# A decoder block in fp32 on one core: keys and values of both halves made in one go and kept, heads in runs of sixteen, and a reordered opening

## What is computed

```python
x = _rmsnorm(hidden_states, ln_weight)
h_q = (x @ w_q.T).reshape(b, lq, H, DH)             # H = 32 heads, DH = 128
h_k = (key_value_states @ w_k.T).reshape(b, lk, H, DH)
h_v = (key_value_states @ w_v.T).reshape(b, lk, H, DH)
score = einsum('bqhd,bkhd->bhqk', h_q, h_k) + position_bias[None]
score = softmax(where(mask, score, -inf))
attn = einsum('bhqk,bkhd->bqhd', where(mask, score, 0), h_v).reshape(b, lq, H * DH)
return hidden_states + attn @ w_out.T
```

## Time and profile before

| | us |
|---|---|
| median of 3 runs (lowest, highest) | 774.87 (773.89, 776.28) |
| profiled execution | 773.13 |
| its span, first to last instruction | 771.3 |
| PE busy | 733.8 |
| PE weight loads busy | 578.8 |
| DVE busy | 487.1 |
| ACT busy | 399.8 |
| POOL busy | 94.9 |
| attention, about | 224 to 630 |

### The profile page before, as it was taken

How to read it: one execution, slowest core, us unless ns; L and a number is a source line. 1 busy time by engine, 2 the same in 40 slices (tenths; PEclk the granted TensorE clock), 3 DMA queues, 4 the chain that set the end, 5 groups by cost and what they waited for, 6 DMA issues and landing times.

```text
span 771.3 us, 12243 instructions
## 1 busy us (share of the span) xinstructions
PE 733.8 (95%) x4320; PEld 578.8 (75%) x4320; DVE 487.1 (63%) x841; ACT 399.8 (52%) x617; POOL 94.9 (12%) x86
## 2 busy tenths in 40 slices
PE   6999999999987999999999999999999889998993
PEld 4887888888877777777777777777776547886882
DVE  5655687577762657665576575765557737578555
ACT  5433333333345666666676656665666454554452
POOL 2010000082009000000000031000000002204503
PEclk9999999999999999999999999999999999999997
DMA  8456532546646677676776777766775333532641
GB/s 328 133 208 212 176 110 82 164 164 193 215 154 213 223 241 247 217 221 223 248 242 194 224 227 234 248 219 226 223 234 174 107 100 124 163 122 97 209 130 55
DMA packets 61335, 145.08 MB, mean 188 GB/s; under 512 B 6896, under 2 KB 6912, under 8 KB 60640
## 3 DMA queue, kind: packets, MB, share of 16 engines
q1 hardware_dynamic: 59696, 136.73, 54.9%
q0 software_dynamic: 1360, 7.23, 2.4%
q10 hardware_dynamic: 224, 0.39, 0.2%
HBM read 142.23 MB, written 2.10 MB: 187 GB/s over the span
## 4 chain that ended last, share of the span: by engine, by line
PE 87%; DVE 4%; DMA 3%; ACT 2%; issue 2%; POOL 1%; SPq 0%; ACTq 0%; DVEq 0%; POOLq 0%
PE bank L475 24%; PE acc L475 15%; PE bank L593 8%; PE acc L728 8%; PE bank L647 7%; PE bank L706 7%; PE bank L612 7%; PE bank L689 7%; DMA a_raw<-a 2%; PE bank L507 1%; PE bank L625 1%; DMA ak<-ax 1%; DVE a_lo L1111 1%; PE bank L673 1%; ACT t_ring L1005 1%
## 5 line engine op out<-in xcount | busy, mean ns | idle before, releaser
L475 PE MATMUL bank<-feat_hi,a_hi 128*128 128x512 f32 x352 | 139.2, 395 | 11.2 <-DVE feat_lo L1111 7.5
L475 PE MATMUL bank<-feat_lo,a_hi 128*128 128x512 f32 x352 | 137.8, 391 | 0.0
L1111 DVE TENSOR_TENSOR a_lo<-a_raw,a_hi 128x1024 fp32r<-128x1024 f32 (+1 forms) x45 | 55.4, 1230 | 99.2 <-ACT a_hi L876 92.8
L1339 DVE TENSOR_TENSOR score<-bank,mask_add 128x512 f32<-128x512 f32 x64 | 42.5, 684 | 114.0 <-PE bank L647 114.0
L593 PEld LDWEIGHTS bank<-few_ctx,ak 128*128 128x128 f32 x512 | 62.0, 191 | 44.6 <-issue 42.4
L475 PE MATMUL acc<-b_hi,tile_hi 128*128 128x512 f32 x224 | 87.7, 392 | 3.6 <-issue 1.9
L1005 ACT ACTIVATE t_ring<-bank 128x512 f32<-128x512 f32 x64 | 69.9, 1092 | 38.0 <-PE bank L612 38.0
L475 PEld LDWEIGHTS bank<-feat_hi,a_hi 128*128 128x128 f32 x352 | 66.6, 189 | 29.1 <-DVE a_lo L1111 10.0
L475 PE MATMUL acc<-b_hi,tile_lo 128*128 128x512 f32 x224 | 87.2, 389 | 0.0
L612 PEld LDWEIGHTS bank<-k_ring,wq 128*128 128x128 f32 x512 | 65.6, 192 | 25.2 <-issue 20.1
L475 PEld LDWEIGHTS bank<-feat_lo,a_hi 128*128 128x128 f32 x352 | 66.6, 189 | 13.6
(11 more groups left out here) (117 smaller groups left out, 1165.7 us busy)
## 6 DMA issues: line engine op xcount, KB each, us to landing
ak<-ax SPq DMA_DIRECT2D x64, 512.0 KB, 3.7
wq<-wqn SPq DMA_DIRECT2D x64, 256.0 KB, 3.9
wv<-wvh SPq DMA_DIRECT2D x64, 256.0 KB, 3.2
wo<-bx SPq DMA_DIRECT2D x64, 256.0 KB, 3.6
a_raw<-w SPq DMA_DIRECT2D x22, 512.0 KB, 4.2
a_raw<-a SPq DMA_DIRECT2D x21, 512.0 KB, 5.3
b_raw<-b SPq DMA_DIRECT2D x34, 256.0 KB, 2.7
b_raw<-w SPq DMA_DIRECT2D x22, 256.0 KB, 2.7
```

The costliest lines, as they stand in the source:

```text
L475: mm = pe.matmul(out_ap, w, x, start=start and k == 0, stop=stop and k == len(products) - 1, skip_group_check=True)
L1111: return dve.tensor_tensor(out_ap, whole, high, ALU.subtract)
L1339: dve.tensor_tensor(score[n % GH][:], bank[2][:].rearrange("p (b k) -> p b k", b=HB), mask_add[j][:, half * HB:(half + 1) * HB, :], ALU.ad ...
```

## The change

Heads run in four runs of sixteen: half 0 with heads 0 to 15, half 1 with heads 0 to 15 and then 16 to 31, half 0 with heads 16 to 31. In the first and third run (`shared`) keys and values are made for both halves at once, as three fp32r products of 256 columns instead of float32 ones of 128; the other half's are kept (`kept_k`, `kept_v`) and used sixteen heads later. In the second and fourth run PE makes none and only raises their semaphores; ACT still copies the banks.

```diff
+BLOCK = HEADS // 2
+WO_RING = 4
+FEATURES_1, FEATURES_2 = BLOCK - LEAD_T - 2, HN - 2
...
+def half_of(n):
+    return (0, 1, 1, 0)[n // BLOCK]
+def head_of(n):
+    return n % BLOCK + (0, 0, BLOCK, BLOCK)[n // BLOCK]
+def shared(n):
+    return n // BLOCK % 2 == 0
...
+ATTENDED = {2: BLOCK, 3: 3 * BLOCK, 4: HN}
...
+        kept_v = [sb(f"kept_v{i}", [P, P])[:] for i in range(BLOCK)]
+        wk_lo, wk_hi = [t[:] for t in two("wk_lo", [P, D], F32R)], [t[:] for t in two("wk_hi", [P, D], F32R)]
...
+        wqi, wk, wo = two("wqi", [P, D]), two("wk", [P, D]), [sb(f"wo{i}", [P, D]) for i in range(WO_RING)]
...
+        few_hi, few_lo = [t[:].rearrange("p w c k -> p (w c k)").rearrange("p (c k) -> p c k", c=C) for t in (a_hi[0], a_lo[0])]
+        wv_hi, wv_lo = [t[:] for t in b_hi], [t[:] for t in b_lo]
+        kept_k = [t[:, i:i + P] for t in (a_raw[1], b_raw[0], b_raw[1]) for i in range(0, t.shape[1], P)]
```

The context rows of both halves come as one tile into `a_raw[0]` and are split into `few_hi`, `few_lo`. The weights w_k and w_v of a shared head are split by ACT and DVE; the loads and their places change:

```diff
+            def load_q(n):
                 if n >= 2:
                     sp.wait_ge(t_mm, n - 1)
-                sp.dma_start(ak[n % 2][:], ax[n % HEADS]).then_inc(ak_dma[n % 2], 16)
-                sp.dma_start(wq[n % 2][:], wqn[n % HEADS]).then_inc(wq_dma[n % 2], 16)
+                sp.dma_start(wqi[n % 2][:], ax[head_of(n)][:, 0:D]).then_inc(wqi_dma[n % 2], 16)
+                sp.dma_start(wq[n % 2][:], wqn[head_of(n)]).then_inc(wq_dma[n % 2], 16)
+            def load_k(n):
+                if n >= 2:
+                    sp.wait_ge(k_mm, n - 1)
+                sp.dma_start(wk[n % 2][:], ax[head_of(n)][:, D:]).then_inc(wk_dma[n % 2], 16)
...
-                if n >= 2:
-                    sp.wait_ge(out_used, n - 1)
-                sp.dma_start(wo[n % 2][:], bx[n % HEADS]).then_inc(wo_dma[n % 2], 16)
...
+                if n >= WO_RING:
+                    sp.wait_ge(out_used, n - WO_RING + 1)
+                sp.dma_start(wo[n % WO_RING][:], bx[head_of(n)]).then_inc(wo_dma[n % WO_RING], 16)
...
             for n in range(2):
-                load_qk(n)
+                load_k(n)
+                load_q(n)
                 load_v(n)
                 load_o(n)
                 load_bias(n)
-            load_a(A30, A30 % 2, w3[0][:, 0:2 * D])
+            sp.wait_ge(a_lo_ok, A30)
+            sp.dma_start(a_raw[0][:], ctxF).then_inc(few_dma, 16)
+            for n in range(2, WO_RING):
+                load_o(n)
...
             for n in range(-LEAD_K, HN):
-                if 2 <= n + LEAD_K + 1 < HN:
-                    load_qk(n + LEAD_K + 1)
-                if n >= 2:
-                    load_o(n)
+                if 2 <= n + LEAD_T + 2 < HN:
+                    load_q(n + LEAD_T + 2)
+                if 2 <= n + LEAD_K + 2 < HN:
+                    load_k(n + LEAD_K + 2)
+                if WO_RING <= n + 2 < HN:
+                    load_o(n + 2)
                 if 2 <= n + 2 < HN:
                     load_v(n + 2)
+                if n == 2 * BLOCK:
+                    sp.wait_ge(few_lo_ok, 1)
+                    load_a(A30, A30 % 2, w3[0][:, 0:2 * D])
...
+            sp.wait_ge(t_mm, HN)
```

PE's keys, values (the same with `wv` and bank 3) and order in an iteration:

```diff
                 def keys(n):
-                    half, par = n // HEADS, n % 2
-                    pe.wait_ge(ak_dma[par], 16 * (n // 2 + 1))
+                    half, par = half_of(n), n % 2
+                    pe.wait_ge(wk_dma[par], 16 * (n // 2 + 1))
+                    if shared(n):
+                        pe.wait_ge(few_lo_ok, 1)
+                        pe.wait_ge(wk_lo_ok, shared_count(n))
                     if n == 0:
                         pe.wait_ge(hidden_ok, HALVES * F1)
                     else:
                         pe.wait_ge(k_ok, n)
+                        pe.wait_ge(kept_k_ok, shared_count(n - 1))
                     if n > LEAD_K + 1:
                         pe.wait_ge(u_ok, n - LEAD_K - 1)
+                    if few and not shared(n):
+                        pe.sem_inc(k_mm, 1)
+                        return
                     for c in range(C):
-                        mm = pe.matmul(bank[1][:, 0:P] if few else bank[1][:], ak[par][:, (C + c) * P:(C + c + 1) * P],
-                                       few_ctx[half][:, c * P:(c + 1) * P] if few else ctx_raw[half][:, c * N:(c + 1) * N],
-                                       start=(c == 0), stop=(c == C - 1))
+                        chunk = slice(c * P, (c + 1) * P)
+                        if few:
+                            mm = passes(bank[1][:, 0:HALVES * P], wk_hi[par][:, chunk], wk_lo[par][:, chunk],
+                                        few_hi[:, c, :], few_lo[:, c, :], c == 0, c == C - 1)
+                        else:
+                            mm = pe.matmul(bank[1][:], wk[par][:, chunk], ctx_raw[half][:, c * N:(c + 1) * N],
+                                           start=(c == 0), stop=(c == C - 1))
                     mm.then_inc(k_mm, 1)
...
+                    if shared(n):
+                        few_keys = k_ring[:, n % RING, half * P:(half + 1) * P]
+                    else:
+                        pe.wait_ge(kept_k_ok, shared_count(n - BLOCK))
+                        few_keys = kept_k[n % BLOCK]
                     for c in range(C):
                         if few:
-                            mm = pe.matmul(bank[0][:, c * P:(c + 1) * P], wq[par][:, c * P:(c + 1) * P], k_ring[:, n % RING, 0:P],
+                            mm = pe.matmul(bank[0][:, c * P:(c + 1) * P], wq[par][:, c * P:(c + 1) * P], few_keys,
...
+                    late = 0 <= n < HN and not shared(n)
+                    if late and n + LEAD_K < HN:
+                        keys(n + LEAD_K)
...
                     if n == -LEAD_K:
                         down(T30 - 1, (T30 - 1) % 2, 1, last=True)
+                    if late:
+                        outer(n - 1)
                     if 0 <= n < HN:
                         values(n)
                     if n == FEATURES_1 or n == FEATURES_1 + 1:
                         features(1, 2 * (n - FEATURES_1) + 1, normed, n + LEAD_T + 1)
...
+                    if n >= 1 and not late:
                         outer(n - 1)
                     if few and j == 2 and g + 1 < HALVES * GROUPS and n >= -2:
```

```diff
+            def split_few():
+                act.wait_ge(few_dma, 16)
+                act.wait_ge(a_used, 2 * A1 - 1)
+                act.activation(a_hi[0][:].rearrange("p w c k -> p (w c k)"), a_raw[0][:], ACT.Copy).then_inc(few_hi_ok, 1)
+            def split_k(n):
+                act.wait_ge(wk_dma[n % 2], 16 * (n // 2 + 1))
+                if n >= 2:
+                    act.wait_ge(k_mm, n - 1)
+                act.activation(wk_hi[n % 2], wk[n % 2][:], ACT.Copy).then_inc(wk_hi_ok, 1)
+            def split_v(n):
+                act.wait_ge(wv_dma[n % 2], 16 * (n // 2 + 1))
+                if n >= 2:
+                    act.wait_ge(v_mm, n - 1)
+                else:
+                    act.wait_ge(b_used, T30)
+                act.activation(wv_hi[n % 2], wv[n % 2][:], ACT.Copy).then_inc(wv_hi_ok, 1)
             def few_bias_heads():
...
+                if shared(n):
+                    other = 1 - half_of(n)
+                    if n >= BLOCK:
+                        act.wait_ge(t_mm, n - BLOCK + 1)
+                    act.activation(kept_k[n % BLOCK], bank[1][:, other * P:(other + 1) * P], ACT.Copy).then_inc(kept_k_ok, 1)
```

The opening loads the first 64 KB of weights by themselves, puts mask and `ad` behind the second half of x on POOL's queue, and PE starts with nine products of a zero tile and then takes each piece as it comes:

```diff
+                    for _ in range(9):
+                        pe.matmul(bank[3][:, 0:P], idle, idle, start=True, stop=True)
                     for c in range(C):
+                        pe.wait_ge(stage_hi_ok, c + 1)
+                        if c == 0:
+                            pe.wait_ge(first_hi_ok, 1)
+                        if c == 1:
+                            pe.wait_ge(a_hi_ok, 1)
+                        pe.matmul(bank[0][:], a_hi[0][:, 0, c, :], feat_hi[0][:, c, :], start=(c == 0), stop=False,
+                                  skip_group_check=True)
+                        if c == 0:
+                            pe.wait_ge(first_lo_ok, 1)
+                        if c == 1:
+                            pe.wait_ge(a_lo_ok, 1)
+                        pe.matmul(bank[0][:], a_lo[0][:, 0, c, :], feat_hi[0][:, c, :], start=False, stop=False,
+                                  skip_group_check=True)
                         pe.wait_ge(stage_lo_ok, c + 1)
-                        mm = passes(bank[0][:], a_hi[0][:, 0, c, :], a_lo[0][:, 0, c, :],
-                                    feat_hi[0][:, c, :], feat_lo[0][:, c, :], c == 0, c == C - 1)
+                        mm = pe.matmul(bank[0][:], a_hi[0][:, 0, c, :], feat_lo[0][:, c, :], start=False, stop=(c == C - 1),
+                                       skip_group_check=True)
                     mm.then_inc(first_mm, 1)
```

More of the change, by code:

```diff
@@ L714, in weigh @@
                 def weigh(n):
[L717 to L718 removed]
+                    part = {0: 2, BLOCK: 3, 3 * BLOCK: 4}.get(n)
```

(3 more changed lines are left out.)

253 lines of the change are left out of this document (161 added, 92 removed).

## The result

The changed kernel takes 781.28 us at the median (779.72 to 781.39, 4 runs) beside 774.38 us for the kernel before on the same chip: ratio 1.0089, 95% interval 1.0076 to 1.0102. It is 0.9% slower where I forecast 1.0% faster. Its profiled execution has a span of 779.4 us, 8.1 more than before.

What follows compares the result with a forecast made beforehand. PE was taken as the bound (87% of the chain), with DVE taking over in late runs. Attention −13.5, edges +5.2, start +2.0 and opening −1.5 gave −7.8 us: 774.87 to 767.1, forecast range 763 to 772.5, low 757, high 780.

Steps and rivals of the forecast that it cites:

- Price of a product: Keys and values of shared heads: each fp32r product of 256 columns costs 0.1165 us, between 0.113 and 0.120.
- Rivals 1 and 2: Shared blocks: products at 0.133 us, 779.8 us, chance 0.13; or fp32r weight loads not overlapping each other, 823 us, chance 0.03.
- Groups of shared heads, +4.0 each: Iterations 0 to 7 and 32 to 39, keys and values both heavy: +4.0 us per group of four, +16.0 in all.
- late runs on DVE's ring, −4.7 each: Iterations 16 to 23 and 48 to 55: DVE's chain limits groups of four to 19.3 us, −4.7 each, −18.9 in all.
- the weigh behind the accumulators: Iterations 16 and 48: the next head's weigh waits for DVE reading the accumulators, about 2.0 us late, twice, +4.0.
- shared heads bound by PE and not by ACT: Iterations 0 to 7 and 32 to 39: ACT works about 5.5 of 7.0 us a head, so PE still bounds.
- 12 to 15 and 44 to 47: +2.0 − 4.0: Iterations with values heavy and keys gone: +2.0 − 4.0 us a group, −4.0 for both groups.
- 24 to 31, −2.7 and −1.6: Iterations 24 to 27: DVE's ring plus two heavy keys, −2.7 us; 28 to 31: values gone, keys heavy, PE-bound, −1.6.
- Start of attention, +2.0: First keys wait for an ACT split and a DVE rest, next ones for weight loads: +2.0 us, ends 0 and +4.
- in the place and size of the weight tile that stood there: 0: Start of attention: context rows load on SP behind twelve loads, where a weight tile stood, and cost 0 us.
- Rival 3: Late blocks miss DVE's ring because of load bursts or ACT's order: 774.9 us, between 772.5 and 777, chance 0.14.
- Opening, −1.5: Kernel start: idle products fill the wait and the first chunk is worked on as it comes, −1.5 us.

Runs made afterwards that it cites:

- e6: e3_pad without the third product of the keys made for both halves (part of the computation left out): 765.78 us, ratio 0.9890, 12.4 us below e3_pad.
- e9: e3_pad without the multiplication of reciprocal row sums by the valid-row flag (part of the computation left out): 772.02 us, ratio 0.9977, 6.2 us below e3_pad.
- e4: Changed kernel with VectorE making the rest of wk ahead of the division instead of behind it, n = 25 to 31: 779.57 us, ratio 1.0057.
- e5: Changed kernel with the context's last rows split behind the previous block's last tile, and the last down projection ahead of the first keys: 779.80 us, ratio 1.0079.
- b5_opening_only: Kernel before with the new opening alone; keys, values and order of heads as before: 773.77 us, ratio 0.9995.
- e11_no_opening: Changed kernel with the old opening, and 42 products in the branch not taken to place the code: 779.02 us, 0.8 more than e3_pad.
- e3_pad: Changed kernel with 24 products added in the branch not taken, moving the code behind it; no executed instruction changed: 778.23 us, ratio 1.0052.
- b10_pad: Kernel before with 106 products added in the branch not taken, giving the changed kernel's code place; no executed instruction changed: 777.74 us, ratio 1.0047.
- e7_all: Changed kernel with turned copies earlier, rest of wk earlier, e5's start, ring keys copied first and 24 products in the branch not taken: 769.37 us, ratio 0.9939.
- e2_start: Changed kernel with the last down projection ahead of the first keys, and ring keys copied ahead of the kept ones: 780.27 us, ratio 1.0073.
- e1_turned_first: Changed kernel with ScalarE copying the turned probabilities ahead of the queries where keys are gone and values heavy: 777.68 us, ratio 1.0031.

## Why the prediction was wrong

The forecast was −7.8 us and +6.9 came, 14.7 us apart. In the trace the keys taken out of iterations 12 to 15 and 44 to 47 are 4.6 us of that, iterations 24 to 31 are 4.5, the start of attention 4.3 and the part behind attention 3.6. Only the last lies outside what the change computes.

- **Price of a product**, 0.1165 taken, 0.120 measured: the upper end of my own bound, the one with the cost over the columns taken as fixed. It did no harm, as I had rounded +0.41 and +0.50 up to +0.5 for keys and values both. Rivals 1 and 2 fall: each of these products has a full weight load of its own (189 ns recorded), and they follow each other every 0.12 us. By the 262 cycles that the Trainium skill gives for 256 columns (page "TensorE: Matmul & The Clock Gate", section "Back-to-back issue gap") it would be an estimated 109 ns. By the rule in "Part 3: Packing small matmuls — row/col tiling" of the same page of the Trainium skill, that a load overlaps products in flight only when it is for other rows, it would be the load plus the columns. The trace, with 120 ns, agrees with neither, and it decides.
- **Groups of shared heads, +4.0 each; late runs on DVE's ring, −4.7 each (19.45 us instead of 24.03); the weigh behind the accumulators; shared heads bound by PE and not by ACT**: right, each within 0.5 us. e6 and e9 show from both sides what bounds which run.
- **"12 to 15 and 44 to 47: +2.0 − 4.0"**: the failed step. I took the keys out of PE's time and did not ask what their 0.99 us had covered. Turns 43 to 47 gained nothing (24.13 against 24.03, where 22.0 was forecast), and seven waits of 0.63 us for ACT's copy of the turned probabilities cost 4.4 us in the two places. I had counted ACT's busy time per iteration and not walked through its order.
- **24 to 31, −2.7 and −1.6**: almost none of it came. Turns 23 to 31 should have lost 5.1 us beside the features that moved away, and lost 0.7. The keys depend on a DVE operation in a strict order behind a wait for scores. I had seen that DVE had the time, not where the operation stands in its row. e4 gives 2 of the missing 4.5 us back; the rest stays open. A small slip of mine is in it: the terms for 24 to 27 add up to 21.4 to 21.6 us and not to 21.3.
- **Start of attention, +2.0**: +7.3 with iteration 0, against 3.0 (+5.8 to +8.6 in the six profiles with this order). That the context rows come "in the place and size of the weight tile that stood there: 0" was the step: the place is the same, the deadline is not. The tile was needed after attention, the rows are needed at once, and ACT waits 3.43 us for them ahead of other work. PE then waits 3.50 us, and its first twelve keys behind that take 2.70 us instead of 1.52 (granted clock 0.72 from 222 to 228 us). Another order at this place brings the first queries 1.4 to 4.2 us forward in the traces (e5 against the six) and the median down by 1.5; the heavier first keys are the likely remainder.
- **Rival 3**, late runs held up by order or loads, had the right kind of cause and the wrong stretch: order cost time where runs of one kind meet the other, not inside the late runs. Its 774.9 is not what came.
- **Opening, −1.5**: the trace has −2.6 up to attention (−1.0 to −2.6 in the nine profiles with both changes, −0.5 in b5_opening_only, and −0.8 in e11_no_opening without it, so about −1.0 is the opening's), the medians 0 to 1.
- **The part behind attention, 0**: +3.6 us, the place of the code. No row of before could show it, and no rival had it. Without it the changed kernel is 0.5% slower (e3_pad), so it decides the size and not the sign.

## What to carry to other kernels

When work is taken off the bounding engine, list what it covered: which copy on another engine was under way while it ran, and what in that engine's row stands ahead of it. A sum of busy time finds the pace of a steady run (all of these were right here); the seams between runs and the first use of each new operand have to be walked in order. And compare two versions with the place of the code held fixed, or a few microseconds of a taken branch count as a result.

## What the runs showed of the hardware

- Behind the branch that is taken, TensorE stood still for 2.1 to 3.3 us, three products in, in the six kernels whose code begins at place 206, and in none of the seven others. Between the changed kernel and e3_pad, and between the kernel before and b10_pad, no executed instruction differs. With the lower clock behind it the gap costs 3.1 and 4.0 us in the medians, and turn 64 to the end is 3.6 to 5.3 us longer in the six traces. Windows of the changed kernel, then of e3_pad:

```profile
640.00:650.00 10.00, 6.48 (x21) 4.82 (x22) 3.14 (x5) 2.68 (x4) 0.00 (x0) 0.83 0.22 80
```

```profile
640.00:650.00 10.00, 8.82 (x39) 6.95 (x39) 6.61 (x9) 5.05 (x7) 0.00 (x0) 1.00 0.34 104
```

- Stretches at 1.2 GHz (a granted clock of 0.50 from 582 to 584 us in the changed kernel) appear in and right behind the late runs, and cost 1.5 to 1.6 us each. PE had short waits before them: 0.71 and 1.01 us for DVE in the changed kernel, 1.43 us for DVE at one place of e7_all, three of 0.2 us at the other. Windows of the changed kernel at such a place (PE busy 4.44 of 6 us, then a granted clock of 0.72):

```profile
574.00:580.00 6.00, 4.44 (x26) 2.34 (x25) 5.83 (x11) 6.00 (x11) 1.98 (x1) 1.00 0.85 277
580.00:586.00 6.00, 5.15 (x20) 2.47 (x21) 3.67 (x8) 2.82 (x5) 0.00 (x0) 0.72 0.86 281
586.00:590.00 4.00, 4.00 (x40) 3.88 (x38) 0.02 (x1) 2.24 (x4) 0.00 (x0) 1.00 0.30 99
```

  Turn 54 to 55 takes 8.92 us here and in e3_pad, 7.28 in e2_start and e1_turned_first; other profiles have one such place in the late runs, or two, or none. The same waits stand in traces without it (0.70 and 1.01 us in e1_turned_first, 1.43 in e4_rest_k), so in this case they are followed by a lower clock in some executions and not in others.
- At the start of attention the last down projection took 2.82 us in the changed kernel and 4.18 in e1_turned_first, with the same code, both behind a wait of 3.5 us (granted clock 0.96 and 0.91 from 222 to 260).
